# Routed attention: the products with the values, one query tile of both images at a time, two steps behind its transposes

## The chip, the cores and the metric

The kernel runs on one core of one Trainium2 chip. The metric is the device time of one execution, in microseconds. TensorE (PE; its weight loads are listed apart as PEld), VectorE (DVE), ScalarE (ACT), GpSimd (POOL) and SyncE (SP) each run their own instructions in order and wait for one another through semaphores.

## The reference, cut to what matters

The input is two images of 32 x 32 tokens with 64 channels. Three parts follow each other: a block of neighbourhood attention with its feed-forward part, a global attention with eight heads, and 33 steps that a router picks from. Only the last part matters here.

```python
def step(h, p):
    op = jnp.argmax(h[0, 0, :NOPS])
    q = h @ p['wq'][op]
    k = h @ p['wk'][op]
    v = h @ p['wv'][op]
    attn = jax.nn.softmax(jnp.einsum('bqd,bkd->bqk', q, k) * scale, axis=-1)
    y = jnp.einsum('bqk,bkd->bqd', attn, v) @ p['wo'][op]
    h = jnp.where(p['am'][op], y, h)
    z = jax.nn.relu(h @ p['w1'][op] + p['b1'][op]) @ p['w2'][op] + p['b2'][op]
    h = jnp.where(p['fm'][op], z, h)
    return (h, None)
```

A step in which neither mask is set leaves h as it is, and the kernel passes over it. With these inputs the router runs one step with the feed-forward part alone, and one with the attention and the feed-forward part. So the routed attention is computed once in an execution: one head of 64 channels, 1024 queries and 1024 keys, for each of the two images.

## The kernel before, in words

The routed attention works on 16 **units**. Unit u is one tile of 128 queries of one image against all 1024 keys: g = u // 8 is the group (the half of 512 queries, since GRP = 8), the lane u % 2 is the image, and (u % 8) // 2 is the query tile in its group. So units 2p and 2p + 1 are the same query tile of the two images. The three functions `pe_attention` (L471), `act_attention` (L988) and `dve_attention` (L1335) hold the order in which TensorE, ScalarE and VectorE work, each as a loop over i that is written out in full by the Python code.

In its step i TensorE computes the scores of unit i + 2 (L483: four float16 matmuls into two PSUM banks), then transposes the probabilities of unit i - 1 (`turn`, L495: four 128 x 128 float32 transposes into bank LO and four into HI), then, in some steps, a part of the products with the values (`values`, L499 to L510) and the product with the output weights (`y_of`, L920 to L929, matmul L928). VectorE in its step i reduces the scores of unit i to their maximum (L1341), inverts the sum of the exponentials of unit i - 1 (L1346), scales its probabilities (L1350), copies HI of unit i - 2 to PT (L1356) and, in some steps, copies the output product from the bank YB to aT (`y_out`, L1733 to L1737). ScalarE in its step i takes the exponentials of unit i (L996), copies LO of unit i - 2 to PT (L1002) and, in some steps, copies the summed output OB to OT (L1007).

`values(g, k)` multiplies 128 keys (number k of 8) with the probabilities of all 512 queries of group g: one matmul for each image, 128 x 64 values as weights and 128 x 512 probabilities moving. The two images have their own half of the PE columns. Each float32 matmul of this kind is two LDWEIGHTS and two MATMUL instructions in the trace. It needs all eight units of its group. The eight k are summed in OB, one PSUM bank, so that a group's output is there only when the last k is done.

The lags say in which step a part of group g comes, counted from step 8g: `LAG_PV` = 10 for the first k (one in each step, the last two together), `LAG_OUT` = 18 for the copy of OB on ScalarE, `LAG_Y` = 19 for `y_of` of both images on TensorE, `LAG_YD` = 22 for both `y_out` on VectorE. All four output products use the one bank YB (bank 7), and each waits until VectorE has copied the one before it (`y_drained`, L926). After the attention come the feed-forward matmuls (L955, L966), which need all four copies: ScalarE's next work waits for the fourth (L1217).

Of the kernel before, what the change touches and what calls it, by code (L numbers as in the profile page):

```python
# [37 lines left out]
P = 128  # L38
B, HH, WW, C = 2, 32, 32, 64
TOK = HH * WW  # L40
NT = TOK // P
BLK = 512
# [16 lines left out]
GRP = 8  # L59
QT = BLK // P  # L60
# [40 lines left out]
FILL = 256  # L101


LAG_PV, LAG_OUT, LAG_Y, LAG_YD = 10, 18, 19, 22


def build(nc, a, out):
    ctx = ExitStack()
    with ctx:
# [7 lines left out]
        PS = ctx.enter_context(nc.psum_tensor("PS", [P, 8, 512], F32))  # L117
        LO, HI, OB, YB = PS[:, 4, :], PS[:, 5, :], PS[:, 6, :], PS[:, 7, :]
# [51 lines left out]
        aT = sb("aT", [C, B * TOK])  # L170
# [5 lines left out]
        V = sb("V", [P, B * NT, P])  # L176
# [61 lines left out]
        gate = sem("gate")  # L238
# [66 lines left out]


        N2 = dict(y=B * NB)
        NF = dict(lo=B * NB + 2, hi=B * NB + 2)

        def nat_drain(copy, func, bank, u):  # L310
# [160 lines left out]
        def pe_attention(pe, s, base, ngroups, y_of):  # L471

            n = GRP * ngroups
            bu, bg = base(n), base(ngroups)

            def score(u):
                g, lane, qt = u // GRP, u % 2, (u % GRP) // 2
                if u >= 2:
                    pe.wait_ge(s["exped"], bu + (u - 1))
                q0 = (g * QT + qt) * P  # L480
                for part in range(2):
                    for j in range(NB):
                        mm = pe.matmul(scores2[u % 2][:, j * BLK:(j + 1) * BLK], qS[:, part, lane, q0:q0 + P],  # L483
                                       kS[:, lane, j * BLK:(j + 1) * BLK], start=(part == 0), stop=(part == 1))
                mm.then_inc(s["scored"], 1)

            def turn(u):
                pe.wait_ge(s["scaled"], bu + (u + 1))
                for half, bank, filled, drained in ((0, LO, "lo_turned", "lo_drained"),
                                                    (1, HI, "hi_turned", "hi_drained")):  # L490
                    if u >= 1:
                        pe.wait_ge(s[drained], bu + u)
                    for k in range(4):
                        kt = 4 * half + k
                        tr = pe.transpose(bank[:, k * P:(k + 1) * P],  # L495
                                          prob[:, u % 3, kt * P:(kt + 1) * P], ident[:, :])
                    tr.then_inc(s[filled], 1)

            def values(g, k):  # L499
                if k == 0:  # L500
                    pe.wait_ge(s["lo_drained"], bu + GRP * (g + 1))
                    pe.wait_ge(s["hi_drained"], bu + GRP * (g + 1))
                    if g >= 1:
                        pe.wait_ge(s["out_drained"], bg + g)
                for lane in range(2):
                    cols = slice(64 * lane, 64 * lane + 64)
                    mm = pe.matmul(OB[64 * lane:64 * lane + 64, :], V[:, (g // 2) * NT + k, cols],  # L507
                                   PT[:, g % 2, lane, k, :], start=(k == 0), stop=(k == NT - 1))
                if k == NT - 1:
                    mm.then_inc(s["out_summed"], 1)  # L510

            score(0)
            score(1)
            for i in range(n + LAG_Y + 3):
                if i + 2 < n:
                    score(i + 2)
                if 1 <= i <= n:
                    turn(i - 1)
                for g in range(ngroups):
                    k = i - GRP * g - LAG_PV  # L520
                    if 0 <= k < NT - 1:
                        values(g, k)
                    if k == NT - 2:
                        values(g, NT - 1)
                    if i == GRP * g + LAG_Y:
                        pe.wait_ge(s["out_drained"], bg + (g + 1))
                        y_of(g, bg)

        @block.tensor
        def _(pe):  # L530
# [363 lines left out]
            def attend(na, step, slot):  # L894
                base = lambda k: pe.snap(na * k)
                bp, bf, by = base(N_SPLIT), base(len(ROUTED)), base(N2["y"])
                for n in range(len(ROUTED)):

                    if n == 0 or n >= 4:
                        pe.wait_ge(routed_split, bp + (4 if n == 0 else 4 + n - 3))  # L900
                        pe.sem_inc(gate, 1)
                    what, lane, blk = ROUTED[n]
                    bank = PS[:, n % 4, :]
                    if what == "v":
                        for j in range(QT):
                            for lane in range(2):
                                t0 = lane * TOK + (blk * QT + j) * P
                                for part in range(2):
                                    m = pe.matmul(bank[:, j * P + C * lane:j * P + C * lane + C], hS[:, t0:t0 + P],
                                                  wsS[:, part, 2, 0, :], start=(part == 0), stop=(part == 1))  # L910
                    else:
                        t0 = lane * TOK + blk * BLK
                        for part in range(2):
                            w = wsS[:, part, "kq".index(what)].rearrange("p a c -> p (a c)")
                            m = pe.matmul(bank, w, hS[:, t0:t0 + BLK], start=(part == 0), stop=(part == 1))
                    m.then_inc(routed_filled, 1)
                pe.wait_ge(routed_split, bp + N_SPLIT)
                pe.sem_inc(gate, 1)

                def y_of(g, bg):  # L920
                    for lane in range(2):
                        n = 2 * g + lane
                        if n == 0:
                            pe.wait_ge(wo_loaded, base(32) + 32)
                        if n:
                            pe.wait_ge(c2["y_drained"], by + n)  # L926
                        pe.sem_inc(gate, 1)
                        pe.matmul(YB[0:C, :], wos[64 * lane:64 * lane + 64, :], OT[64 * lane:64 * lane + 64, g % 2, :],  # L928
                                  start=True, stop=True).then_inc(c2["y_filled"], 1)  # L929

                pe_attention(pe, c2, base, 2, y_of)
                pe.wait_ge(c2["y_drained"], by + 4)
                pe.sem_inc(gate, 1)
# [401 lines left out]
        def dve_attention(dve, s, base, ngroups, y_out):  # L1335
            n = GRP * ngroups
            bu, bg = base(n), base(ngroups)
            for i in range(n + LAG_YD + 2):
                if i < n:
                    dve.wait_ge(s["scored"], bu + (i + 1))  # L1340
                    dve.tensor_reduce(negm[:, i % 4:i % 4 + 1], scores2[i % 2], AX.X, ALU.max, negate=True)\  # L1341
                       .then_inc(s["maxed"], 1)
                if 1 <= i <= n:
                    u = i - 1
                    dve.wait_ge(s["exped"], bu + (u + 1))
                    dve.reciprocal(rinv[:, u % 4:u % 4 + 1], rsum[:, u % 4:u % 4 + 1]).then_inc(s["inverted"], 1)  # L1346
                if 1 <= i <= n:
                    u = i - 1
                    dve.wait_ge(s["inverted"], bu + (u + 1))
                    dve.tensor_scalar(prob[:, u % 3, :], prob[:, u % 3, :], rinv[:, u % 4:u % 4 + 1], None,  # L1350
                                      ALU.mult).then_inc(s["scaled"], 1)
                u = i - 2
                if 0 <= u < n:
                    g, lane, qt = u // GRP, u % 2, (u % GRP) // 2
                    dve.wait_ge(s["hi_turned"], bu + (u + 1))
                    dve.tensor_copy(PT[:, g % 2, lane, 4:8, qt * P:(qt + 1) * P],  # L1356
                                    HI.rearrange("p (k q) -> p k q", k=4)).then_inc(s["hi_drained"], 1)
                for g in range(ngroups):
                    if i == GRP * g + LAG_YD:
                        y_out(g, bg)  # L1360

        @block.vector
        def _(dve):
# [357 lines left out]
            def attend(na, step, slot):  # L1721
# [8 lines left out]
                    dve.wait_ge(routed_high, bp + (4 + n + 1))  # L1730
                    low_part(piece, PS[:, n % 4, :], (1.0, C ** -0.5), routed_split)

                def y_out(g, bg):  # L1733
                    for lane in range(2):
                        dve.wait_ge(c2["y_filled"], by + (2 * g + lane + 1))
                        dve.tensor_copy(aT[:, lane * TOK + g * BLK:lane * TOK + (g + 1) * BLK], YB[0:C, :])\
                           .then_inc(c2["y_drained"], 1)  # L1737
                dve_attention(dve, c2, base, 2, y_out)

            def feed(nf, step, slot):  # L1740
# [115 lines left out]
```

## Time and profile before

| what | value |
|---|---|
| median of 3 runs | 734.24 us |
| the three runs | 734.24, 734.43, 728.93 us |
| the profiled execution | 730.25 us |
| its span, first to last instruction | 728.4 us |
| mean granted TensorE clock in it | 0.944 of full |
| TensorE busy in it | 87% of the span |

The span covers the three parts one after the other. The routed attention is the stretch from 634.67 us (its first score matmul) to about 697.2 us (its last copy). Times in the trace's rows count from the start of the span. A row of a timeline merges like instructions that follow one another: where it starts, how long it lasts, engine, line, operation, output and input, shape, and how often; in square brackets the engine's idle time before it and what ended it. Since matmuls are pipelined, the time of a single row holds the end of the last matmul, which the next matmul overlaps: the distance from one start to the next is what an operation costs the engine.

### The profile page before, as it was taken

How to read it: one execution, taken by the hardware profiler on the slowest of the kernel's cores; microseconds unless marked ns; L12 is line 12 of the kernel's file. 1: busy time of each engine (PE TensorE's matmuls, PEld its weight loads, DVE VectorE, ACT ScalarE, POOL GpSimd, SP SyncE). 2: the span in 40 equal slices, each digit the busy share in tenths (PEclk: the TensorE clock that was granted, in tenths of full speed). 3: DMA queues.
4: the chain of work that ended last, by engine and by line, in shares of the span. 5: the costliest groups of instructions: out<-in, count | busy, mean ns of one | idle time of the engine just before them, and what ended most of it. 6: DMA issues, size and time to landing. Idle time of an engine off the chain costs nothing.

```text
span 728.4 us, 10696 instructions
## 1 busy us (share of the span) xinstructions
PE 631.9 (87%) x3759; PEld 336.4 (46%) x3760; DVE 465.0 (64%) x799; ACT 386.4 (53%) x683; POOL 50.2 (7%) x100
## 2 busy tenths in 40 slices
PE   7999999869699999999999999999998725478862
PEld 5555655535445555555555555555554311244311
DVE  5655464655866767677666766676768545699343
ACT  3544558335666666666575666566655022466130
POOL 5021323220000000000000000000000000000000
PEclk9999999957999999999999999999999867799986
DMA  4000000000000000000000000000000000000001
GB/s 96 1 1 1 2 1 1 1 0 1 1 1 1 0 1 1 1 1 1 1 0 0 0 0 0 0 1 1 1 0 1 1 10 1 12 1 1 1 0 29
DMA packets 9507, 3.21 MB, mean 4 GB/s; under 512 B 8820, under 2 KB 9079, under 8 KB 9463
## 3 DMA queue, kind: packets, MB, share of 16 engines
q1 hardware_dynamic: 8182, 2.61, 1.5%
q8 instruction: 28, 0.46, 0.3%
q10 hardware_dynamic: 1281, 0.01, 0.1%
q14 instruction: 16, 0.13, 0.1%
HBM read 2.09 MB, written 0.52 MB: 4 GB/s over the span
## 4 chain that ended last, share of the span: by engine, by line
PE 73%; DVE 12%; issue 9%; ACT 2%; POOL 2%; DMA 1%; SPq 0%; DVEq 0%; POOLq 0%; ACTq 0%
PE PS L829 15%; PE PS L802 15%; PE PS L815 13%; PE PS L656 3%; PE PS L670 3%; PE PS L683 2%; PE PS L855 2%; PE PS L483 2%; PE PS L762 2%; PE PS L495 2%; PE PS L507 2%; PE PS L697 2%; PE PS L955 2%; DVE negm L1604 2%; PE PS L556 1%
## 5 line engine op out<-in xcount | busy, mean ns | idle before, releaser
L1604 DVE TENSOR_REDUCE negm<-PS 128x1 f32<-128x1024 f32 x128 | 156.6, 1223 | 119.7 <-PE PS L802 119.6
L1164 ACT ACTIVATE prob<-PS,negm 128x1024 f32<-128x1024 f32 x128 | 142.8, 1116 | 43.4 <-DVE negm L1604 43.4
L815 PE MATMUL PS<-ident,prob 128*128 128x128 f32 x1024 | 135.8, 274 | 10.5 <-DVE PT L1616 10.3
L815 PEld LDWEIGHTS PS<-ident,prob 128*128 128x128 f32 x1024 | 119.7, 141 | 39.0 <-DVE PT L1616 13.3
L829 PE MATMUL PS<-PT,V 128*64 128x512 f32 x512 | 134.4, 617 | 0.0
L802 PE MATMUL PS<-aS,qS 128*128 128x512 f16 x512 | 133.8, 384 | 0.0
L1176 ACT ACTIVATE PT<-PS 128x512 f32<-128x512 f32 x128 | 76.6, 598 | 106.4 <-PE PS L815 105.8
L1616 DVE COPY PT<-PS 128x512 f32<-128x512 f32 x128 | 87.2, 681 | 4.7 <-PE PS L815 4.7
L802 PEld LDWEIGHTS PS<-aS,qS 128*128 128x128 f16 x512 | 44.5, 99 | 95.9 <-issue 52.1
L1093 ACT ACTIVATE prob<-sbias,negm 128x320 f32<-128x320 f32 (+1 forms) x64 | 34.3, 537 | 36.9 <-DVE negm L1516 36.4
L1283 POOL TENSOR_TENSOR rstd<-var,minus_half 128x8 f32<-128x8 f32 x8 | 13.2, 1645 | 467.1 <-DVE var L1387 467.1
L656 PE MATMUL PS<-ident 128*128 128x256 f16 x128 | 38.5, 301 | 5.5 <-DVE negm L1516 4.0
L829 PEld LDWEIGHTS PS<-PT,V 128*64 128x64 f32 x512 | 27.3, 135 | 30.0 <-issue 29.8
L314 DVE COPY PT<-PS 128x384 f32<-128x384 f32 (+1 forms) x32 | 16.7, 523 | 31.7 <-PE PS L683 31.7
L1516 DVE CUSTOM_DVE_ANT_0 sbias<-PS,PT 128x320 f32<-128x320 f32 (+1 forms) x64 | 28.7, 458 | 6.8 <-PE PS L670 6.8
L683 PE MATMUL PS<-ident,prob 128*128 128x128 f32 x176 | 32.4, 292 | 0.0
L670 PE MATMUL PS<-k0S,q0S 32*128 32x320 f16 (+1 forms) x128 | 29.9, 317 | 0.0
L656 PEld LDWEIGHTS PS<-ident 128*128 128x128 f16 x128 | 13.0, 101 | 32.8 <-issue 16.2
L996 ACT ACTIVATE prob<-PS,negm 128x1024 f32<-128x1024 f32 x16 | 17.8, 1114 | 16.7 <-DVE negm L1341 16.7
L1164 ACT ACTIVATION_READ_ACCUMULATOR prob<-PS,negm 128x1 f32 x128 | 25.3, 198 | 0.0
L1138 ACT ACTIVATE qS<-PS 128x512 f16<-128x512 f32 x36 | 21.2, 598 | 7.7 <-PE PS L762 7.4
L483 PE MATMUL PS<-kS,qS 128*128 128x512 f16 x64 | 16.4, 381 | 9.0 <-ACT prob L996 7.7
(175 smaller groups left out, 677.9 us busy)
## 6 DMA issues: line engine op xcount, KB each, us to landing
xall<-in_x_dram SPq DMA_DIRECT2D x2, 256.0 KB, 4.4
out_dram<-x SPq DMA_DIRECT2D x4, 128.0 KB, 2.1
w<-in_L_attn_Wq_dram SPq DMA_DIRECT2D x2, 128.0 KB, 2.5
w<-in_L_attn_Wk_dram SPq DMA_DIRECT2D x2, 128.0 KB, 2.8
w<-in_L_attn_Wv_dram SPq DMA_DIRECT2D x2, 128.0 KB, 2.6
fc<-in_L_conv_fc_w_dram SPq DMA_DIRECT2D x2, 64.0 KB, 2.5
wu<-in_L_attn_Wu_dram SPq DMA_DIRECT2D x2, 64.0 KB, 2.4
w1s<-in_L_ffn_ffn_w_dram SPq DMA_DIRECT2D x2, 64.0 KB, 2.1
```

The source lines that it names most:

```text
L483: mm = pe.matmul(scores2[u % 2][:, j * BLK:(j + 1) * BLK], qS[:, part, lane, q0:q0 + P], kS[:, lane, j * BLK:(j + 1) * BLK], start=(part = ...
L656: pe.matmul(bank[:, 0:FILL], filler[:, 0:P], filler[:, 0:FILL], start=True, stop=True)
L670: mm = pe.matmul(PS[:, u % 2, 0:rows * WW], q0S[hr, img, part, t * P:(t + 1) * P], k0S[hr, img, first * WW:(first + rows) * WW], start=(pa ...
L683: tr = pe.transpose(bank[:, n * P:(n + 1) * P], prob[:, u % 3, n * P:(n + 1) * P], ident[:, :])
L802: mm = pe.matmul(scores2[i % 2][:, j * BLK:(j + 1) * BLK], qS[:, part, lane, q0:q0 + P], aS[:, k0 + j * BLK:k0 + (j + 1) * BLK], start=(pa ...
L815: tr = pe.transpose(bank[:, k * P:(k + 1) * P], prob[:, u % 4, kt * P:(kt + 1) * P], ident[:, :])
L829: mm = pe.matmul(OB[cols, :], V[:, g % GP // 2 * NT + kt, cols], PT[:, g % 2, lane, kt, :], start=(kt == 0), stop=(kt == NT - 1))
L1093: act.activation(prob[:, i % 3, 0:w], sbias[:, i % 3, 0:w], ACT.Exp, bias=negm[:, i % 4:i % 4 + 1], scale=-1.0).then_inc(c0["exped"], 1)
L1164: act.activation(prob[:, i % 4, :], scores2[i % 2], ACT.Exp, bias=negm[:, i % 4:i % 4 + 1], scale=1.0, accum_out=sums[:, i // GRP, (i % GR ...
L1176: act.activation(PT[:, g % 2, lane, 0:4, qt * P:(qt + 1) * P], LO.rearrange("p (k q) -> p k q", k=4), ACT.Copy).then_inc(c1["lo_drained"], 1)
L1604: dve.tensor_reduce(negm[:, i % 4:i % 4 + 1], scores2[i % 2], AX.X, ALU.max, negate=True)\
L1616: dve.tensor_copy(PT[:, g % 2, lane, 4:8, qt * P:(qt + 1) * P], HI.rearrange("p (k q) -> p k q", k=4)).then_inc(c1["hi_drained"], 1)
```

## The change

The constants become `LAG_PV, LAG_OUT, LAG_Y, LAG_YD` = 3, 11, 11, 12. `values(p, half)` now takes the pair p of units 2p and 2p + 1, one query tile of both images, and half of the eight key tiles: four k, for each of them one matmul of 128 moving columns for each image. The eight k of a query tile are summed in its quarter of OB. Step i issues `values((i - 3) // 2, (i - 3) % 2)` for i from 3 to 18. `y_of` and `y_out` do one image in a step, in two steps after each other, and `y_of` now stands behind `values` in the step. The fourth output product goes to bank 0 of PSUM, which the scores no longer use by then, and waits for no copy.

```diff
-LAG_PV, LAG_OUT, LAG_Y, LAG_YD = 10, 18, 19, 22
+LAG_PV, LAG_OUT, LAG_Y, LAG_YD = 3, 11, 11, 12
...
+        def y_bank(n):
+
+            return PS[:, 0, :] if n == N2["y"] - 1 else YB
...
-            def values(g, k):
-                if k == 0:
-                    pe.wait_ge(s["lo_drained"], bu + GRP * (g + 1))
-                    pe.wait_ge(s["hi_drained"], bu + GRP * (g + 1))
-                    if g >= 1:
+            def values(p, half):
+
+                g, qt = p // QT, p % QT
+                if half == 0:
+                    pe.wait_ge(s["lo_drained"], bu + 2 * (p + 1))
+                    pe.wait_ge(s["hi_drained"], bu + 2 * (p + 1))
+                    if g >= 1 and qt == 0:
                         pe.wait_ge(s["out_drained"], bg + g)
-                for lane in range(2):
-                    cols = slice(64 * lane, 64 * lane + 64)
-                    mm = pe.matmul(OB[64 * lane:64 * lane + 64, :], V[:, (g // 2) * NT + k, cols],
-                                   PT[:, g % 2, lane, k, :], start=(k == 0), stop=(k == NT - 1))
-                if k == NT - 1:
+                toks = slice(qt * P, (qt + 1) * P)
+                for k in range(NT // 2 * half, NT // 2 * (half + 1)):
+                    for lane in range(2):
+                        cols = slice(64 * lane, 64 * lane + 64)
+                        mm = pe.matmul(OB[cols, toks], V[:, (g // 2) * NT + k, cols],
+                                       PT[:, g % 2, lane, k, toks], start=(k == 0), stop=(k == NT - 1))
+                if half == 1 and qt == QT - 1:
                     mm.then_inc(s["out_summed"], 1)
...
+                if 0 <= i - LAG_PV < n:
+                    values((i - LAG_PV) // 2, (i - LAG_PV) % 2)
                 for g in range(ngroups):
-                    k = i - GRP * g - LAG_PV
-                    if 0 <= k < NT - 1:
-                        values(g, k)
-                    if k == NT - 2:
-                        values(g, NT - 1)
-                    if i == GRP * g + LAG_Y:
+                    if i - GRP * g - LAG_Y in range(2):
                         pe.wait_ge(s["out_drained"], bg + (g + 1))
-                        y_of(g, bg)
+                        y_of(g, i - GRP * g - LAG_Y)
...
+                def y_of(g, lane):
+                    n = 2 * g + lane
+                    if n == 0:
+                        pe.wait_ge(wo_loaded, base(32) + 32)
+                    if 0 < n < N2["y"] - 1:
+                        pe.wait_ge(c2["y_drained"], by + n)
+                    pe.sem_inc(gate, 1)
+                    pe.matmul(y_bank(n)[0:C, :], wos[64 * lane:64 * lane + 64, :], OT[64 * lane:64 * lane + 64, g % 2, :],
+                              start=True, stop=True).then_inc(c2["y_filled"], 1)
...
-                    if i == GRP * g + LAG_YD:
-                        y_out(g, bg)
+                    if i - GRP * g - LAG_YD in range(2):
+                        y_out(g, i - GRP * g - LAG_YD)
...
+                def y_out(g, lane):
+                    dve.wait_ge(c2["y_filled"], by + (2 * g + lane + 1))
+                    dve.tensor_copy(aT[:, lane * TOK + g * BLK:lane * TOK + (g + 1) * BLK],
+                                    y_bank(2 * g + lane)[0:C, :]).then_inc(c2["y_drained"], 1)
```

## Rows read from the trace of the kernel before

**Rows 1.** The page: busy time and share of engines; granted TensorE clock in 40 slices.

```profile
PE 631.9 (87%) x3759; PEld 336.4 (46%) x3760; DVE 465.0 (64%) x799; ACT 386.4 (53%) x683; POOL 50.2 (7%) x100
PEclk9999999957999999999999999999999867799986
```

**Rows 2.** Busy time by stretch of the routed attention: length, each engine, clock, DMA.

```profile
634.70:644.40 9.70, 6.71 (x36) 3.46 (x36) 8.28 (x12) 5.24 (x10) 0.00 (x0) 1.00 0.01 2
644.40:662.60 18.20, 13.41 (x85) 8.76 (x86) 17.95 (x29) 11.92 (x22) 0.00 (x0) 1.00 0.00 0
662.60:681.70 19.10, 18.41 (x104) 9.19 (x104) 15.38 (x25) 10.05 (x18) 0.00 (x0) 1.00 0.00 1
681.70:697.20 15.50, 11.39 (x42) 2.87 (x40) 2.72 (x4) 1.19 (x2) 0.00 (x0) 1.00 0.00 1
```

**Rows 3.** Timeline, a step without values: VectorE's four operations, then TensorE's next scores.

```profile
641.94 1.22 DVE L1341 TENSOR_REDUCE negm<-PS 128x1 f32<-128x1024 f32 x1
643.07 0.15 DVE L1346 RECIPROCAL rinv<-rsum 128x1 f32<-128x1 f32 x1
643.26 0.75 DVE L1350 TENSOR_SCALAR prob<-prob,rinv 128x1024 f32<-128x1024 f32 x1
643.93 0.68 DVE L1356 COPY PT<-PS 128x512 f32<-128x512 f32 x1
...
644.45 1.04 PE L483 MATMUL PS<-kS,qS 128*128 128x512 f16 x4 [0.69 <-ACT prob L996]
```

**Rows 4.** Timeline, steps with values: TensorE's three parts, then VectorE's copy and reduction.

```profile
668.27 1.04 PE L483 MATMUL PS<-kS,qS 128*128 128x512 f16 x4
...
669.15 1.04 PE L495 MATMUL PS<-ident,prob 128*128 128x128 f32 x8
...
670.11 1.08 PE L507 MATMUL PS<-PT,V 128*64 128x512 f32 x4
...
671.12 1.04 PE L483 MATMUL PS<-kS,qS 128*128 128x512 f16 x4
...
673.07 0.69 DVE L1356 COPY PT<-PS 128x512 f32<-128x512 f32 x1 [0.17 <-PE PS L495]
...
673.68 1.22 DVE L1341 TENSOR_REDUCE negm<-PS 128x1 f32<-128x1024 f32 x1
```

**Rows 5.** Timeline of the tail, from the transposes of unit 14 to the last copy.

```profile
676.77 1.06 PE L495 MATMUL PS<-ident,prob 128*128 128x128 f32 x8 [0.69 <-ACT PT L1002]
...
679.79 1.94 PE L507 MATMUL PS<-PT,V 128*64 128x512 f32 x8
...
685.37 1.04 PE L928 MATMUL PS<-OT,wos 64*64 64x512 f32 x2 [0.87 <-DVE aT L1736]
686.34 6.23 PE L507 MATMUL PS<-PT,V 128*64 128x512 f32 x28
...
692.62 0.60 ACT L1007 ACTIVATE OT<-PS 128x512 f32<-128x512 f32 x1 [10.24 <-PE PS L507]
...
693.54 1.04 PE L928 MATMUL PS<-OT,wos 64*64 64x512 f32 x2 [0.97 <-ACT OT L1007]
...
695.45 1.04 PE L928 MATMUL PS<-OT,wos 64*64 64x512 f32 x2 [0.87 <-DVE aT L1736]
696.53 0.68 DVE L1736 COPY aT<-PS 64x512 f32<-64x512 f32 x1 [1.23 <-PE PS L928]
```

**Rows 6.** Timelines elsewhere: float32 matmuls of 128 moving columns and their weight loads.

```profile
108.84 0.38 PEld L697 LDWEIGHTS PS<-PT 128*32 128x32 f32 x16 [0.17 <-ACT PT L314]
...
431.09 1.16 PE L855 MATMUL PS<-wu,OT 128*128 x8
```

**Rows 7.** Feed-forward matmuls behind the attention, and the granted clock of that stretch.

```profile
699.92 6.23 PE L955 MATMUL PS<-aS,w1S 128*128 128x512 f16 x14 [3.42 <-DVE aS L1719]
...
700.00:707.00 7.00, 6.64 (x16) 1.12 (x15) 3.83 (x6) 3.36 (x6) 0.00 (x0) 0.63 0.00 0
```

**Rows 8.** Instruction groups by line: weight loads of the products with the values.

```profile
L507 PEld LDWEIGHTS PS<-PT,V 128*64 128x64 f32 x64 | 3.8, 136 | 7.6 <-issue 6.0 <-ACT OT L1007 1.6
```

More of the change, by code:

```diff
@@ L918, in attend @@
                 pe.sem_inc(gate, 1)
[L920 to L929, printed above, removed]
+                def y_of(g, lane):
[7 more added lines that the diff above has]
+                              start=True, stop=True).then_inc(c2["y_filled"], 1)
                 pe_attention(pe, c2, base, 2, y_of)
@@ L1731, in attend @@
                     low_part(piece, PS[:, n % 4, :], (1.0, C ** -0.5), routed_split)
[L1733 to L1737, printed above, removed]
+                def y_out(g, lane):
+                    dve.wait_ge(c2["y_filled"], by + (2 * g + lane + 1))
+                    dve.tensor_copy(aT[:, lane * TOK + g * BLK:lane * TOK + (g + 1) * BLK],
+                                    y_bank(2 * g + lane)[0:C, :]).then_inc(c2["y_drained"], 1)
                 dve_attention(dve, c2, base, 2, y_out)
```

## The prediction, made before the changed kernel ran

> **What bounds the kernel now.** I read the page first: TensorE is busy 87% of the span and its clock dips only at a few places [rows 1]. That is an average over three parts, and the change touches one stretch of some 62.5 us, so I went to the busy times by stretch [rows 2]. From 644.4 to 662.6 VectorE is busy 17.95 of 18.2 us and TensorE 13.41; from 662.6 to 681.7 TensorE is busy 18.41 of 19.1 us. In the last 15.5 us VectorE works 2.72 us and ScalarE 1.19, while TensorE is alone with products. So there are three stages with three limits, and I read the timeline of each.
>
> In a step without values VectorE has no gap [rows 3]: maximum, inverse, scaling and copy take 1.13 + 0.19 + 0.67 + 0.6 = 2.59 us, and TensorE idles 0.69 us of them. In a step with values TensorE has none [rows 4]: scores 0.88 us (668.27 to 669.15), transposes 0.96, one k of the values 1.01 (670.11 to 671.12), in sum 2.85 us. VectorE now waits for TensorE (the 0.17 before its copy). In the tail [rows 5] the values of group 0 end and those of group 1 begin to run alone: 28 matmuls last 6.23 us; then come the copy of OB, an output product, its copy, the second product at 695.45 and its copy to 697.21. The second product waited 0.87 us for the first one's copy.
>
> **What is removed from the tail.** Before, the transposes of unit 14 start at 676.77 and the last copy ends at 697.21: 20.44 us [rows 5]. After the change, the same transposes are followed by: 3.02 us up to the values behind the transposes of unit 15 (676.77 to 679.79, the same order of work), then three halves of values in a row. Each half is four k, each k two pairs of matmuls (a pair is the two images, which run beside each other in their halves of the array), so 24 pairs. The 28 instructions before are 14 pairs in 6.23 us; 8 instructions (4 pairs) took 1.94; the difference, 4.29 us over 10 pairs, is 0.429 us for a pair of 512 columns, with 0.22 over. A quarter of the columns is 0.107; I take 0.109. Three halves are then 24 x 0.109 + 0.22 = 2.84 us. The last copies of the 16 units are ready in time: a copy of HI ends 1.76 us after the start of its unit's transposes (672.00 to 673.76, where 672.00 is 671.12 + 0.88) [rows 4], and the values that need the one of unit 15 start 0.96 + 0.9 us after it. Then 0.05 us to the copy of OB, 0.92 to the first output product (692.62 to 693.54), 0.97 to the second, which waits for nothing now (a product costs TensorE 0.97: 685.37 to 686.34), 1.08 to its copy and 0.68 for it. Sum: 3.02 + 2.84 + 0.05 + 0.92 + 0.97 + 1.08 + 0.68 = 9.56 us. Removed: 20.44 - 9.56 = 10.9 us.
>
> **What is added ahead of it.** First, values in steps 3 to 9, where there were none. A half is 8 pairs, 8 x 0.109 = 0.87 us, and changing between these and the other matmuls costs what it does now: 1.01 - 2 x 0.429 = 0.15. That is 1.02 us in place of 1.01, so a step is 0.88 + 0.96 + 1.02 = 2.86 us, longer than VectorE's 2.59. Seven steps by 0.27 make 1.9 us: the idle 0.69 of TensorE [rows 3] hides the rest. Four more steps cost 0.01 each. Their wait for the copies adds nothing, since the transposes just ahead of them have waited for the same copies.
>
> Second, the two output products of group 0 move from the tail into steps 11 and 12, where TensorE is full: 2 x 0.97 = 1.94 us.
>
> Third, a new wait. VectorE's copy of the first of these products stands in its step 12, but the product is issued at the end of TensorE's step 11, behind the values. Counting from the start of TensorE's step 11: scores to 0.88, transposes to 1.84, values to 2.86, product readable at 2.86 + 1.08 = 3.94, copy and next operation at 4.6. Behind that copy in VectorE's queue stands the maximum of unit 13, which before began 2.56 us after that point; ScalarE's exponential waits for it, and ScalarE's copy of LO stands behind the exponential. TensorE's step 12 starts at 3.83 and its product is readable at 7.75, so the maximum of unit 14 starts at 8.4 instead of 5.4. Then come VectorE's 2.59 us to the maximum of unit 15 at 11.0, and from that maximum to the start of the transposes of unit 14 (over its exponential and the copy of LO behind it) 3.09 us, as now (673.68 to 676.77): 14.1 us. Before, that was 11.35 (676.77 less 665.42, one step ahead of 668.27). The difference is 2.75 us: 1.94 of products and 0.8 of late maxima.
>
> Added in all: 1.9 + 0.05 + 1.94 + 0.8 = 4.7 us. **Net: 10.9 - 4.7 = 6.2 us less.** The copy of OB on ScalarE costs nothing, as ScalarE idles (18.2 - 11.92) / 7 = 0.9 us in each step [rows 2]; without that cover it would cost 0.6. No DMA is issued or moved, and SP's and POOL's queues are untouched. The extra 96 pairs are 192 LDWEIGHTS and 192 MATMUL instructions; fetching them shows in no row, and I take nothing for it: in the short products elsewhere 16 loads are issued in 0.38 us [rows 6], faster than the change asks. A stall would cost at least the 0.69 of slack in one step before it shows.
>
> Against its own time the profiled execution would go from 730.25 to 724.05. The median shown, 734.24, is 4 us above it, since two runs stand at 734.3 and one at 728.9. The gain taken from the median gives **728.0 us**, 0.85% less. About 1% is what a measurement of this kernel can tell from no change.
>
> **The price that no row shows.** The values of before never load weights for only 128 columns: 64 loads of 0.136 us [rows 8] lie under 0.429 us of matmul. From below, a pair can't be under 0.107. From above: eight matmuls of 128 columns with 128 x 128 loads take 1.16 us in all [rows 6], at most 0.145 each, and eight transposes take 0.96, 0.12 each [rows 4]. At 0.145 the 128 pairs cost 128 x 0.036 = 4.6 us more. I take 0.109, since the 16 loads in 0.38 us are the nearest shape (several column groups at once) and leave 0.1 us for a group of four.
>
> The 28 value matmuls of the tail take 0.429 us for each pair, with their loads wholly hidden, although all of them use all 128 rows [rows 5]. The Trainium skill (TensorE: Matmul & The Clock Gate, Part 3, The mechanism) says that LDWEIGHTS overlaps running matmuls only when the row group differs; by that rule no load here would be hidden. With that page's load time of columns / 1.2 ns (section LDWEIGHTS), an estimate is 53 ns by 128 pairs, 6.8 us, and the result 734.8. The trace speaks against it.
>
> **The rivals.** *Loads exposed (slower).* If at 128 columns a load no longer hides, a pair costs up to 0.109 + 0.136 us, and 128 pairs cost 17.4 us more: 745.4 us. It decides at 6.2 / 128 = 0.048 us a pair for no gain, and at 0.105 for slower by 1%. For it: the load row is longer than the matmul it must hide under [rows 8]. Against it: transposes and short products run at 0.12 to 0.145 with loads of the same length [rows 4, 6]. A part of it (0.03 to 0.06 a pair) gives 732 to 736.
>
> *The late maxima cost more.* If each of the two products delays VectorE by its full 0.97 + 0.65 with no slack taken up, 3.2 us instead of 2.75: 728.5. Or, with the copies finding room, 1.94 only: 727.2. Both are inside the forecast.
>
> *The feed-forward part runs at another clock.* Behind the attention TensorE idles 3.42 us, and 14 of the next matmuls run in 6.23 us, the clock at 0.63 on average over 7 us [rows 7]: it had fallen to 1.2 GHz. With two output products back to back and no gap the fall may come later or its end sooner. At 2.4 GHz the 14 would take at least half, but their copies pace them too; I bound it by 3.1 us less, and by 1 us more if the end comes later. With the full gain: 724.9, faster by 1.3%.
>
> *The second output product runs beside the first.* They use different rows of the array and now different banks. Then the last copy follows the one before it: 0.3 us less. The Trainium skill (TensorEngine Tiling (Array Packing), Key Properties) says that tiles run independently. No row of before shows it, as the second always waited. 727.7 by that.
>
> **How the numbers follow.** The forecast (6.2 us less, with the small terms) has 0.70; the clock 0.13; loads partly exposed 0.10, wholly exposed 0.07. Since the runs shown differ by 5.5 us among themselves and 6.2 us is only 1.1 short of 1%, the forecast's 0.70 splits into 0.32 faster and 0.38 within 1%; the clock case gives 0.11 faster and 0.02 same, the partial case 0.09 same and 0.01 slower, the full case slower. In sum 0.43 faster, 0.49 within 1%, 0.08 slower. The range goes down to the lower group of runs less the gain (728.93 - 6.2 = 722.7, with 1 us of the clock: 721.7) and up to the upper bound of a pair (728.0 + 4.6, and 1 us of clock: 733.6). What is outside is the wholly exposed load and half of the partial case on one side, and the full clock gain with the lower group on the other.
>
> **What would show each step.** In the changed profile: steps of 2.86 us from step 3 on, TensorE without idle time; halves of 16 matmuls in about 1 us; VectorE's copy of the first output product idle some 1.3 us ahead of it for TensorE, and the transposes of unit 13 waiting about 1 us for ScalarE's copy; the transposes of unit 14 at about 681.4; one run of 48 value matmuls in 2.8 us at the end; the second output product 0.97 us after the first; the last copy at about 691.0. A step of over 3 us without an output product would say that loads are exposed. A feed-forward part of other length than before would speak for the clock. The prediction is wrong if the steps are as said and the end is not, or if the late maxima spread over later steps.

## The result

| | before | after |
|---|---|---|
| median of 5 runs | 729.51 us | 721.35 us |
| the runs | 734.24, 734.43, 728.93, 729.15, 729.51 | 727.60, 721.24, 721.35, 721.23, 722.47 |
| the profiled execution, its span | 730.25 us, 728.4 us | 727.60 us, 725.7 us |
| routed attention, first score matmul to last copy | 62.54 us | 56.01 us |

The ratio of the changed kernel to the one before is 0.9892, with a 95% interval from 0.9847 to 0.9937: 0.6 to 1.5% faster. The forecast was 728.0 us, in a range from 721.7 to 733.6. The measured median lies 0.35 us under that range. Two of the five runs of before came after the three that the prediction had, and they took its median from 734.24 to 729.51. Medians, ratios and ranges of timed runs, here and below, leave out the four runs that took over 1.5% longer than the fastest of the same kernel (731.77 us of the changed kernel; 738.42, 738.91 and 2470.06 us of the one before).

The page of the changed kernel: its span, busy shares, granted TensorE clock in 40 slices.

```profile
span 725.7 us, 11085 instructions
...
PE 636.4 (88%) x3951; PEld 348.2 (48%) x3952; DVE 465.6 (64%) x799; ACT 386.7 (53%) x683; POOL 50.3 (7%) x100
...
PEclk9999999876999999999999999999999886699986
```

TensorE has the 192 matmuls and 192 loads more that the diff adds (3759 and 3760 before, [rows 1]). The line PEclk has a digit for each slice, in tenths of full clock. To see where the 2.7 us between the two spans come from, here is the busy time by stage. The columns are the stretch and its length, busy time and instructions of PE, PEld, DVE, ACT and POOL, then the granted clock. First the kernel before:

```profile
0.00:130.00 130.00, 121.03 (x911) 70.26 (x912) 71.02 (x218) 69.17 (x136) 35.62 (x79) 1.00 0.06 15
130.00:200.00 70.00, 53.80 (x320) 32.36 (x319) 44.91 (x81) 33.40 (x61) 11.28 (x19) 0.83 0.00 1
200.00:590.00 390.00, 375.09 (x2129) 198.25 (x2129) 267.22 (x358) 232.30 (x399) 1.64 (x1) 0.99 0.00 1
590.00:634.70 44.70, 19.20 (x90) 6.83 (x91) 24.22 (x46) 16.02 (x27) 1.64 (x1) 0.67 0.03 6
634.70:697.20 62.50, 49.92 (x264) 24.27 (x264) 44.32 (x68) 28.40 (x50) 0.00 (x0) 1.00 0.00 1
697.20:728.40 31.20, 12.80 (x49) 4.43 (x49) 13.33 (x31) 7.13 (x12) 0.00 (x0) 0.68 0.07 17
```

And the changed kernel, cut where the same work begins and ends:

```profile
0.00:130.00 130.00, 121.03 (x908) 70.02 (x909) 71.00 (x218) 69.01 (x135) 35.71 (x79) 1.00 0.07 15
130.00:203.60 73.60, 57.69 (x323) 34.16 (x321) 45.63 (x84) 34.19 (x61) 11.33 (x19) 0.79 0.00 1
203.60:593.60 390.00, 375.56 (x2129) 198.63 (x2129) 266.74 (x357) 231.99 (x399) 1.64 (x1) 0.99 0.00 1
593.60:638.30 44.70, 19.65 (x90) 6.86 (x91) 24.22 (x46) 15.99 (x27) 1.64 (x1) 0.66 0.03 6
638.30:694.30 56.00, 49.55 (x456) 34.14 (x456) 44.71 (x68) 28.42 (x50) 0.00 (x0) 1.00 0.01 1
694.30:725.70 31.40, 12.89 (x49) 4.43 (x49) 13.32 (x30) 7.14 (x12) 0.00 (x0) 0.68 0.08 17
```

Two stages differ. The routed attention is 6.5 us shorter: TensorE's busy time stays the same (49.92 and 49.55 us) and its idle time falls from 12.6 to 6.5. The stage from 130 us on, whose code the diff doesn't touch, is 3.6 us longer in this execution, at a clock of 0.79 in place of 0.83. The last stage, with the feed-forward part, is as long as before (31.2 and 31.4 us, clock 0.68 both times).

TensorE's steps with values, in the changed kernel's timeline (they answer to [rows 4]):

```profile
659.51 1.04 PE L487 MATMUL PS<-kS,qS 128*128 128x512 f16 x4
660.39 1.04 PE L499 MATMUL PS<-ident,prob 128*128 128x128 f32 x8
661.35 1.09 PE L515 MATMUL PS<-PT,V 128*64 128x128 f32 x16
662.38 1.04 PE L487 MATMUL PS<-kS,qS 128*128 128x512 f16 x4
```

Scores 0.88 us, transposes 0.96, half a query tile's values 1.03 (the wide form took 1.01 for one k): a step of 2.87 us, forecast 2.86, with no gap.

The first output product of group 0 and what stands behind it, then the transposes of units 13 and 14:

```profile
673.84 1.07 PE L932 MATMUL PS<-OT,wos 64*64 64x512 f32 x2
...
674.95 0.68 DVE L1739 COPY aT<-PS 64x512 f32<-64x512 f32 x1 [1.33 <-PE PS L932]
...
675.56 1.21 DVE L1345 TENSOR_REDUCE negm<-PS 128x1 f32<-128x1024 f32 x1
...
682.50 1.06 PE L499 MATMUL PS<-ident,prob 128*128 128x128 f32 x8 [0.85 <-ACT PT L1006]
...
685.09 1.06 PE L499 MATMUL PS<-ident,prob 128*128 128x128 f32 x8 [0.50 <-ACT PT L1006]
```

This is the new wait of the forecast: VectorE stands 1.33 us in front of the copy, the maximum of unit 13 starts only at 675.56, 4.58 us after TensorE's step 11 began at 670.98 (2.56 before the change, 671.12 to 673.68 for the step and the maximum in [rows 4]), and TensorE pays for it at the transposes of unit 13, where it waits 0.85 us. From the first score to the transposes of unit 14 it is now 685.09 - 638.27 = 46.82 us; it was 676.77 - 634.67 = 42.10. Added: 4.7 us, forecast 4.7.

The tail (answers to [rows 5]):

```profile
688.13 2.67 PEld L515 LDWEIGHTS PS<-PT,V 128*64 128x64 f32 x48 [0.17 <-issue]
688.14 2.91 PE L515 MATMUL PS<-PT,V 128*64 128x128 f32 x48
...
691.09 0.60 ACT L1011 ACTIVATE OT<-PS 128x512 f32<-128x512 f32 x1 [2.68 <-PE PS L515]
...
691.92 1.19 PE L932 MATMUL PS<-OT,wos 64*64 64x512 f32 x4 [0.87 <-ACT OT L1011]
693.00 1.28 DVE L1739 COPY aT<-PS 64x512 f32<-64x512 f32 x2 [4.06 <-PE PS L932]
```

The 48 value matmuls run in one piece of 2.91 us (forecast 2.84), with their 48 loads under them. From 688.30 to 688.95 the starts of the pairs in the trace are 0.109 us apart. The four instructions of the last two output products take 1.19 us in all, where one product alone took 1.04: they ran side by side. The two copies follow each other without a gap. From the transposes of unit 14 to the end it is 9.19 us (forecast 9.56), in place of 20.44. Removed are 11.25 us, added 4.72, and the net is 6.53 us less.

### The profile page after: what moved, and what is told of

It reads as the page before. It is cut to its first block, busy times and chain, and to the rows that moved or that the text cites. A ratio compares the mean times of both kernels' runs of the same rounds, so it can differ in the third digit from the quotient of the medians.

```text
span 725.7 us, 11085 instructions
## 1 busy us (share of the span) xinstructions
PE 636.4 (88%) x3951; PEld 348.2 (48%) x3952; DVE 465.6 (64%) x799; ACT 386.7 (53%) x683; POOL 50.3 (7%) x100
## 4 chain that ended last, share of the span: by engine, by line
PE 74%; DVE 12%; issue 9%; ACT 2%; POOL 2%; DMA 1%; SPq 0%; DVEq 0%; POOLq 0%; ACTq 0%
PE PS L834 16%; PE PS L807 15%; PE PS L820 13%; PE PS L661 3%; PE PS L675 3%; PE PS L688 2%; PE PS L860 2%; PE PS L515 2%; PE PS L767 2%; PE PS L702 2%; PE PS L487 2%; PE PS L959 2%; PE PS L499 2%; DVE negm L1608 2%; PE PS L561 1%
## 5 line engine op out<-in xcount | busy, mean ns | idle before, releaser
L820 PE MATMUL PS<-ident,prob 128*128 128x128 f32 x1024 | 135.9, 274 | 10.5 <-DVE PT L1620 10.3
L661 PE MATMUL PS<-ident 128*128 128x256 f16 x128 | 39.3, 307 | 5.4 <-DVE negm L1520 4.1
L661 PEld LDWEIGHTS PS<-ident 128*128 128x128 f16 x128 | 13.1, 103 | 33.5 <-issue 16.6
L767 PE MATMUL PS<-aS,wqk 128*128 128x512 f16 x64 | 20.4, 414 | 5.0 <-DVE qS L1576 3.6
```

What stands on the lines that cost most here:

```text
L661: pe.matmul(bank[:, 0:FILL], filler[:, 0:P], filler[:, 0:FILL], start=True, stop=True)
L767: m = pe.matmul(bank, w.rearrange("p h a c -> p (h a c)"), aS[:, blk * BLK:(blk + 1) * BLK], start=(part == 0), stop=(part == 1))
L820: tr = pe.transpose(bank[:, k * P:(k + 1) * P], prob[:, u % 4, kt * P:(kt + 1) * P], ident[:, :])
```

## The experiments

Since the executions of one kernel differ by several microseconds, the mechanisms are read from the length of the routed attention in each profiled execution. That length repeats: 62.54 and 62.45 us in two profiles of the kernel before, 56.01 and 56.00 in two of the changed one.

**Both kernels once more.** No edit.

> The changed kernel once more, unchanged. Its profiled execution stood 3.6 us behind the one of before by the start of the routed attention, all of it between 130 us and the end of the second part's start, at a clock of 0.79 against 0.83. Theory A (the change gives 6.5 us, and what lies beyond it in the medians is how the executions fall into groups): the stretch from the first routed score to the last copy is 56.0 us again, the stretch behind it 31.3 to 31.4, and the stage from 130 us on is 70.0 or 73.6 us long depending on the clock; the timed difference lies at 6.5 us where both kernels fall alike, 721.3 or 727.6 us. Theory B (the change gives 8 us): one of the other stretches of a fast execution is 1.4 us shorter than in the profile of before.

> The kernel before, once more, for a second profile. Theory A: 62.5 us for the routed attention and 31.2 us behind it, and a length of the stage from 130 us on that goes with its granted clock. Theory B: the profile of before was 1.4 us longer than its fast executions of 729.2 us in one of the stretches, and this one shows which.

The changed kernel: 723.2 us, median of 11 runs from 718.54 to 727.70, ratio 0.9915 (0.9883 to 0.9947) to 21 runs of the kernel before, whose median is 729.26 and which go from 724.83 to 734.69 us. Its profile: 56.00 us for the attention, 31.4 behind it, and 73.6 us for the stage from 130 us on, at a clock of 0.79. The kernel before had one run, 740.42 us, which was also profiled; a line of its page and the busy times of two stretches of it:

```profile
PEclk9995699986999999999999999999999877699986
...
0.00:140.00 140.00, 131.81 (x892) 75.10 (x894) 70.84 (x216) 68.24 (x133) 35.61 (x79) 0.88 0.06 14
53.10:87.20 34.10, 34.10 (x178) 18.95 (x177) 11.12 (x36) 10.33 (x23) 2.83 (x8) 0.50 0.00 1
```

This span is 10.2 us longer than that of the first profile (738.6 and 728.4), and the routed attention begins 10.3 us later (645.0 and 634.67): all of it lies ahead. TensorE ran at 1.2 GHz from 53.10 to 87.20 us, busy all of that time, where the first profile has full clock [rows 1]. The last gap of TensorE ahead of that, 0.80 us, is in both profiles. First the profile in which the clock then fell, then the one in which it didn't:

```profile
52.65 0.28 PE L656 MATMUL PS<-ident 128*128 128x256 f16 x1 [0.80 <-DVE negm L1516]
...
54.28 0.28 PE L656 MATMUL PS<-ident 128*128 128x256 f16 x1 [0.80 <-DVE negm L1516]
```

The same matmul (L656, L661 in the changed kernel) shows one more difference, ahead of that. In each profile it takes 0.39 to 0.42 us at first, as it does between 53.10 and 87.20 us in this second profile, where the clock is at 1.2 GHz, and 0.27 to 0.28 later, and the moment of the change differs; the line PEclk reads 9 on both sides of it. In the kernel before, then in the run `one_bank` below:

```profile
45.80 0.42 PE L656 MATMUL PS<-ident 128*128 128x256 f16 x1
46.61 0.28 PE L656 MATMUL PS<-ident 128*128 128x256 f16 x1
...
35.79 0.39 PE L661 MATMUL PS<-ident 128*128 128x256 f16 x1
37.73 0.28 PE L661 MATMUL PS<-ident 128*128 128x256 f16 x1
```

For all nine profiles of this case, from the changed kernel (`after`, `again`), the kernel before (`before`, `before_again`) and the versions below: the first fast one of these matmuls, the time that the granted clock is at 1.2 GHz between it and 240 us, and the start of the attention, in us:

| profile | first fast matmul | later at 1.2 GHz | sum | attention starts |
|---|---|---|---|---|
| y_at_17 | 37.75 | 20.48 | 58.23 | 629.05 |
| one_bank | 37.73 | 20.48 | 58.21 | 629.07 |
| y_at_14 | 37.76 | 20.48 | 58.24 | 629.29 |
| before_two_banks | 44.93 | 20.48 | 65.41 | 632.04 |
| y_11_13 | 42.92 | 27.31 | 70.23 | 633.79 |
| before | 46.61 | 23.89 | 70.50 | 634.67 |
| again | 46.71 | 30.72 | 77.43 | 637.87 |
| after | 48.36 | 30.72 | 79.08 | 638.27 |
| before_again | 43.07 | 54.61 | 97.68 | 644.98 |

The start of the attention follows the sum, 15.9 us for 39.5, or some 0.4 us for each, behind work that no edit touches. So nearly all of what differs between the executions ahead of the attention goes with how long TensorE runs at 1.2 GHz in the first 200 us, the 3.6 us between the first two profiles too (sums of 70.50 and 79.08). That agrees with theory A. Theory B wants a stretch that only the change makes shorter, and none was found.

**All output products in one bank again** (`one_bank`).

```diff
-            return PS[:, 0, :] if n == N2["y"] - 1 else YB
+            return YB
...
-                    if 0 < n < N2["y"] - 1:
+                    if n > 0:
```

> The changed kernel with all four output products in bank YB, each behind the copy of the one before it, as before the change. If the second product of the last pair runs beside the first only because it has its own bank: the last copy comes 1.3 us later (1.91 us from the first product to the second, as before, then 1.08 and 0.68, against 2.36 us from the first product to the end of both copies now), 57.3 us for the attention. If the two run beside each other for another reason (the missing wait changes nothing), the same 56.0. Elsewhere nothing: the products of group 0 are steps apart.

724.41 us, median of 10 runs, ratio 0.994 (0.9909 to 0.9971). The end of its timeline:

```profile
682.72 1.04 PE L932 MATMUL PS<-OT,wos 64*64 64x512 f32 x2 [0.87 <-ACT OT L1011]
683.79 0.68 DVE L1739 COPY aT<-PS 64x512 f32<-64x512 f32 x1 [4.06 <-PE PS L932]
...
684.62 1.04 PE L932 MATMUL PS<-OT,wos 64*64 64x512 f32 x2 [0.87 <-DVE aT L1739]
685.70 0.68 DVE L1739 COPY aT<-PS 64x512 f32<-64x512 f32 x1 [1.23 <-PE PS L932]
```

57.31 us for the attention, 1.30 more than the changed kernel: the price named in the expectation. With one bank comes the wait for the copy, so this run doesn't tell the bank from the wait; it shows what the two cost together.

**The products of group 0 further apart** (`y_11_13`).

```diff
-                    if i - GRP * g - LAG_Y in range(2):
-                        pe.wait_ge(s["out_drained"], bg + (g + 1))
-                        y_of(g, i - GRP * g - LAG_Y)
+                    for lane in range(2):
+                        if i == ((11, 13), (19, 20))[g][lane]:
+                            pe.wait_ge(s["out_drained"], bg + (g + 1))
+                            y_of(g, lane)
...
-                    if i - GRP * g - LAG_YD in range(2):
-                        y_out(g, i - GRP * g - LAG_YD)
+                    for lane in range(2):
+                        if i == ((13, 15), (20, 21))[g][lane]:
+                            y_out(g, lane)
```

> The changed kernel with the output products of group 0 on TensorE in steps 11 and 13 in place of 11 and 12, and VectorE's copies of them in steps 13 and 15 in place of 12 and 13, so that each is readable before VectorE comes to it. If the late maxima cost 0.8 us as forecast: 0.8 us less, 55.2 us for the attention, and no wait of VectorE's copy for TensorE (1.33 and 0.59 us now). If the copies themselves (0.65 us each in VectorE's queue) are what delays the maxima: no less than 0.3 us less, 55.7. If the transposes of unit 13 waited for something else: 56.0.

719.8 us, median of 4 runs, ratio 0.9862 (0.9816 to 0.9908). 54.58 us for the attention: 1.43 less, where 0.8 was expected.

```profile
669.05 1.21 DVE L1346 TENSOR_REDUCE negm<-PS 128x1 f32<-128x1024 f32 x1
...
672.31 0.69 DVE L1361 COPY PT<-PS 128x512 f32<-128x512 f32 x1 [1.19 <-PE PS L499]
672.92 0.67 DVE L1741 COPY aT<-PS 64x512 f32<-64x512 f32 x1
...
677.10 1.09 PE L499 MATMUL PS<-ident,prob 128*128 128x128 f32 x8
...
679.18 1.06 PE L499 MATMUL PS<-ident,prob 128*128 128x128 f32 x8
```

VectorE's copy of the product (L1741) has no wait ahead of it. VectorE still stands 1.19 us for TensorE's longer step 11, now ahead of its copy of HI (L1361), but that is behind the maximum of unit 13, which starts at 669.05, 2.55 us after step 11 began at 666.50 (4.58 in the changed kernel). TensorE's transposes of units 13 and 14 have no wait either. In the changed kernel these two waits were 0.85 and 0.50 us, 1.35 of the 1.43 that are gone. So two things went: the late maxima, 0.8 us by the forecast, and also the idle time that TensorE has ahead of the transposes of unit 14, 0.69 us in the kernel before. The second product stands behind the last scores here, delays nothing that VectorE needs for a maximum, and takes the place of that idle time. No expectation had this second effect, and this run alone doesn't divide the 1.43 us between the two.

**Both products of group 0 behind the last scores, side by side** (`y_at_14`).

```diff
-            return PS[:, 0, :] if n == N2["y"] - 1 else YB
+            return PS[:, 0, :] if n % 2 else YB
...
-                    if 0 < n < N2["y"] - 1:
-                        pe.wait_ge(c2["y_drained"], by + n)
+                    if n == 2:
+                        pe.wait_ge(c2["y_drained"], by + 2)
...
-                    if i - GRP * g - LAG_Y in range(2):
+                    if i == (14, 19)[g]:
                         pe.wait_ge(s["out_drained"], bg + (g + 1))
-                        y_of(g, i - GRP * g - LAG_Y)
+                        if g == 0:
+                            pe.wait_ge(s["exped"], bu + 15)
+                        y_of(g, 0)
+                        y_of(g, 1)
...
-                    if i - GRP * g - LAG_YD in range(2):
-                        y_out(g, i - GRP * g - LAG_YD)
+                    for lane in range(2):
+                        if i == ((16, 17), (20, 21))[g][lane]:
+                            y_out(g, lane)
```

The new wait for `exped` keeps bank 0 until ScalarE has read the scores of unit 14 from it.

> The changed kernel with both output products of group 0 in TensorE's step 14, behind the last scores, one in bank YB and one in bank 0, so that they can run beside each other; VectorE copies them in steps 16 and 17. The second pair is in two banks as well. From the rows so far: without the two products in steps 11 and 12 (1.94 us) and without the late maxima (0.8 us) the attention would take 56.0 - 2.7 = 53.3 us, with 0.69 us of TensorE idle ahead of the transposes of unit 14 as in the kernel before. The pair costs 1.15 us side by side, of which that idle time hides 0.69. Theory A (the idle time can be filled, and the pair runs side by side): 53.7 us for the attention, some 8.8 us less than before the change, in time about 2.3 us less than the changed kernel. Theory B (the idle time moves behind the products): 54.4 us.

718.75 us, median of 6 runs, ratio 0.9848 (0.9804 to 0.9891). 53.58 us for the attention (53.7 and 54.4 expected by the two theories).

```profile
672.65 1.08 PE L935 MATMUL PS<-OT,wos 64*64 64x512 f32 x4
673.65 1.09 PE L499 MATMUL PS<-ident,prob 128*128 128x128 f32 x8
...
680.51 1.19 PE L935 MATMUL PS<-OT,wos 64*64 64x512 f32 x4 [0.87 <-ACT OT L1014]
681.59 1.28 DVE L1743 COPY aT<-PS 64x512 f32<-64x512 f32 x2 [3.48 <-PE PS L935]
```

The pair of group 0 costs TensorE 1.00 us for both products, and the transposes behind it wait for nothing. Its median is 11.3 us under the 730.0 us of the 16 runs of before beside it, and it is the lowest of all versions. Of these 11.3 us, 9.0 lie in the attention (62.54 and 53.58); nothing here says where the rest comes from. Its interval overlaps a little with that of the changed kernel's second comparison (0.9883 to 0.9947), so that between these two the attention's 2.4 us speak, not the timed runs.

**The same pair where nothing hides it** (`y_at_17`). Steps 17 and 18 in place of 14, 16 and 17:

```diff
-                    if i == (14, 19)[g]:
+                    if i == (17, 19)[g]:
...
-                        if i == ((16, 17), (20, 21))[g][lane]:
+                        if i == ((18, 18), (20, 21))[g][lane]:
```

> The same with the pair of group 0 in step 17, behind all transposes and one half of values, where nothing hides it. Both theories: 53.3 + 1.15 = 54.4 us for the attention. The difference to the run with the pair in step 14 is what the idle time hides: 0.69 us by theory A, nothing by theory B.

720.09 us, median of 4 runs, ratio 0.9846 (0.9794 to 0.9898). 54.44 us for the attention.

```profile
673.14 1.06 PE L499 MATMUL PS<-ident,prob 128*128 128x128 f32 x8 [0.66 <-ACT PT L1009]
...
678.15 1.08 PE L935 MATMUL PS<-OT,wos 64*64 64x512 f32 x4
679.15 1.09 PE L515 MATMUL PS<-PT,V 128*64 128x128 f32 x16
```

The wait of 0.66 us ahead of unit 14 is back, and the pair costs 1.00 us behind it. The difference in the attention, 0.86 us, is the idle time filled and 0.2 more, so theory A holds for the idle time. The timed runs alone could not tell the two versions apart.

**The kernel before with two banks alone** (`before_two_banks`).

```diff
-                        if n:
-                            pe.wait_ge(c2["y_drained"], by + n)
+                        if n == 2:
+                            pe.wait_ge(c2["y_drained"], by + 2)
                         pe.sem_inc(gate, 1)
-                        pe.matmul(YB[0:C, :], wos[64 * lane:64 * lane + 64, :], OT[64 * lane:64 * lane + 64, g % 2, :],
+                        pe.matmul((YB, PS[:, 0, :])[lane][0:C, :], wos[64 * lane:64 * lane + 64, :], OT[64 * lane:64 * lane + 64, g % 2, :],
...
-                        dve.tensor_copy(aT[:, lane * TOK + g * BLK:lane * TOK + (g + 1) * BLK], YB[0:C, :])\
+                        dve.tensor_copy(aT[:, lane * TOK + g * BLK:lane * TOK + (g + 1) * BLK],
+                                        (YB, PS[:, 0, :])[lane][0:C, :])\
```

> The kernel before with one part of the change alone, and for both groups: the second product of a pair goes to bank 0 and does not wait for the copy of the first. If pairs run side by side in general: group 0 takes TensorE 1.15 us in place of 2.90 (683.44 to 686.34), 1.75 us less, and at the end 1.3 us less, so 62.5 - 3.05 = 59.5 us for the attention. If they run one after the other: 0.97 and 0.95 us less, 60.6. What is then left of the change's 6.5 us, 3.4 or 4.6, is the early start of the values.

726.02 us, median of 10 runs, ratio 0.9956 (0.9917 to 0.9996).

```profile
680.80 1.08 PE L928 MATMUL PS<-OT,wos 64*64 64x512 f32 x4
681.81 6.23 PE L507 MATMUL PS<-PT,V 128*64 128x512 f32 x28
...
688.92 1.19 PE L928 MATMUL PS<-OT,wos 64*64 64x512 f32 x4 [0.88 <-ACT OT L1007]
```

59.24 us for the attention (59.5 for pairs side by side, 60.6 for one after the other): both pairs ran side by side, 1.01 us for the first in place of 2.90. So of the 8.1 us between the kernel before and the version with both products in step 17 (62.54 and 54.44), 3.3 come from the second bank, put in first, and 4.8 from what is then added: the early, narrow values, with the pair of group 0 ahead of the last of them. The changed kernel, at 56.01 us, gives 1.6 of that back, through its products in steps 11 and 12.

## Why the prediction missed

The forecast was right in its mechanism and in nearly all terms of its sum, and wrong in what the sum was subtracted from. The miss of 6.7 us (728.04 and 721.35) divides into 4.7 of the base (734.24 and 729.51), 0.3 of the gain (6.2 and 6.5) and 1.6 that lie outside the attention and that no profile explains.

- **Step of values: right.** 2.87 us against 2.86. The pair of narrow matmuls costs the 0.109 us that was chosen, not the 0.145 of the upper bound: 24 pairs took 2.91 us, 2.84 by the forecast.
- **Loads exposed: refuted.** The steps have no gap, and the 48 matmuls of the tail have their 48 loads under them, all on the same 128 rows. The Trainium skill's rule (TensorE: Matmul & The Clock Gate, Part 3, The mechanism) that a load overlaps running matmuls only in another row group does not hold here: the estimate from it put 6.8 us more on the 128 pairs, and the values of a step took 1.03 us where 1.02 was forecast with hidden loads.
- **The two products in full steps and the late maxima: right.** 4.7 us added, as forecast. A product cost TensorE 1.01 and 1.00 us in its full steps (673.84 to 674.85, 677.71 to 678.71), 0.97 by the forecast. The wait showed at the transposes of unit 13 (0.85 us, 1 us forecast) and moved the one of unit 14 from 0.69 to 0.50. The experiment with the products in steps 11 and 13 removed both waits.
- **Second product beside the first: it was given as a rival of 0.3 us, and it happened.** From the first of the last two products to the end it is 2.36 us, 2.73 by the forecast, and this 0.4 is what separates 6.2 us from the measured 6.5. The Trainium skill (TensorEngine Tiling (Array Packing), Key Properties) says that tiles run independently; the trace agrees, 1.19 us for both at the end.
- **Another clock in the feed-forward part: did not happen.** 31.2 and 31.4 us behind the attention, clock 0.68 in both.
- **The step that failed is the base.** The gain was taken from 734.24 us, a median in which two of three runs lay high. With two runs more the median was 729.51 us, and 21 later runs of the same kernel have 729.26. From 729.51 the forecast's 6.2 us gives 723.3, well inside the range. The prediction said that the runs differ by 5.5 us and spoke of a lower group, and yet set the point in the upper one. The profiled execution, 730.25 us, and the lowest run, 728.93, both lay nearer to the later medians than the median of three did.
- **The low end of the range was too high as well.** It was the lowest of three runs less the gain, 722.7, and 1 us more for the clock of the feed-forward part. With the measured gain, 6.5 us, the lowest of three runs gives 722.4, still 1.1 us above the measured median. The prediction had nothing in its range for how far the executions of one kernel lie apart, beyond its own three runs: the 21 later runs of the kernel before span 9.9 us, and the lowest of them, 724.83, is 4.1 us under the lowest of the three.

Of the 8.2 us between the first medians, 6.5 are in the traces. The other 1.6 are not explained by anything in the attention: they are small beside the 15.9 us by which the start of the attention differs among the nine profiles, but only one of the runs of each kernel was profiled, so no run ties them to it. The second comparison gives 6.1 us (729.26 and 723.20), and 6.5 us of 729.5 is a ratio of 0.991, inside both intervals. Why TensorE runs at 1.2 GHz for longer in the first 200 us of some executions was not tried, and stays open.

## What to carry to other kernels

Before a gain is turned into a time, look at how wide the executions lie, and take the base from all of them, the profiled one too: here the base was off by 4.7 us and the gain by 0.3. In a pipeline written out by hand, look at the queue of the engine that copies a product out, not only at the engine that computes it: a copy put one step too early made VectorE wait 1.33 us and delayed the next maximum by 2 us. Look for work that must be done once, and try it behind the last piece of the repeated work: here the pipeline ran out there and left 0.69 us of idle time, and the two products of group 0 were cheapest in it.

## What the runs showed of the hardware that was not expected

Two float32 output products of 64 x 64 weights and 512 columns, in different halves of the array's rows and into different banks but the same 64 output partitions, take TensorE 1.00 us together (672.65 to 673.65), where one alone takes 1.01 in the same place of a step (673.84 to 674.85) and 0.97 in the tail [rows 5]. Changing the products with the values from 512 to 128 moving columns, which needs four times as many weight loads, cost 0.02 us in a step (1.03 and 1.01 us). And TensorE's granted clock was at 1.2 GHz for 34.1 us in which TensorE had no idle time (53.10 to 87.20), in one execution and not in another of the same kernel, with the same gap of 0.80 us ahead of it in both. The attention began 10.3 us later in that execution. Over nine profiles of seven versions, the time that TensorE ran at 1.2 GHz ahead of it, 58.2 to 97.7 us, goes with nearly all of the 15.9 us by which its start differs.
